# Holding back expert loads until the first gathers have landed, and gathering rows four tiles ahead

## The chip, the cores and the metric

The kernel runs on one core of a Trainium2 chip, as one program launched once. The metric is the device time of that launch in microseconds (us), the median of several runs of the same program on the same inputs. All arrays are in float32 unless a line says otherwise.

## The reference

The input is `x` of shape (2, 1024, 256), which is 2048 tokens of 256 values, with 77 context rows for each of the two sequences. Eight residual steps follow, in four pairs of an attention step and a feed-forward step; each adds its result to `x`, and its input is the layer norm of `x`.

```
x = x + L0_xattn(norm(x), ctx)      # softmax over the queries
x = x + L0_ffn(norm(x))             # dense, with quantised weights and activations
x = x + L1_xattn(norm(x), ctx)      # 16 heads, with its own feed-forward inside
x = x + L1_ffn(norm(x))             # 16-head self-attention, then 8 experts, top 2 of each token
x = x + L2_xattn(norm(x), ctx)
x = x + L2_ffn(norm(x))             # 8 experts, every expert whose sigmoid is over 0.5
x = x + L3_xattn(norm(x), ctx)
x = x + L3_ffn(norm(x))             # 8 experts, the best one of each token
```

An expert is `act(t @ W1 + b1) @ W2 + b2` with W1 of 256x1024 and W2 of 1024x256; its result is multiplied by the token's weight for that expert and summed over the chosen experts.

## The kernel before

Each step is a stage with its own block of instructions on every engine. The change is in one function, `routed_layer`, which runs three times: for the top-2 layer (semaphores and tiles named m1), the threshold layer (m2) and the top-1 layer (m3). Here they are called the first, second and third routed stage.

**Routing.** The normed tokens (16 tiles of 128 tokens) are stored to a table in device memory, `scratch_rows`, by four transfers on SyncE's queue (L1940). TensorE turns the tokens and computes the gate. VectorE picks the experts, computes each token's weight for each expert and, with TensorE, a list of tokens for every expert, cut into tiles of 128 places; the last tile of an expert is filled up with a padding id. ScalarE's queue stores the weights beside the tokens' rows in the same table (L2308, 2048 pieces of 32 bytes). The list of ids lands in the tile `ids` (L2245), which raises `ids_done`.

**The loop over tiles.** Every tile belongs to one expert. Its steps on the engines are:

- GpSimd copies 128 ids into a place of `row_ids` (L1984) and issues an indirect DMA, the gather, that brings 128 rows of the table into a place of `rows`, a ring of four (L1987). For the first tiles this is done ahead of the loop (L2011 and L2015), after GpSimd has waited for `stored`, the landing of all five stores into the table, and for `ids_done`.
- TensorE turns the rows (`transpose_rows`, L2074), VectorE copies them to `rowsT` (L2270, or L2266 with gain and shift in the first stage), TensorE multiplies by W1 (`first`, L2083, 32 instructions), ScalarE applies the activation, TensorE multiplies by W2 (`second`, L2092, and L2095 for the output bias).
- VectorE copies W1 of the next tile's expert (L2255) and the tile's weights (`weight`, which raises `tail_in`, L2274).
- ScalarE scales the result into a place of `y` (L2331, which raises `y_sb`). GpSimd issues an indirect DMA that adds the 128 rows of `y` to the stream in device memory (L1998). An addition is issued only after the one before it has landed (`y_out`).

TensorE's order is written out by hand: `first(s)`, `transpose_rows(s + 1)`, `second(s - 1)`. GpSimd's order is in `add_rows(s)`: wait until addition s - 1 has landed, gather tile s + 3, wait for `y` of tile s, issue addition s. The loop is unrolled over four pairs of tiles and skips the pairs that the routing left empty. There are 38, 68 and 20 tiles in the three stages.

**The experts.** W1 and W2 of an expert are 1 MB each. The first two (first stage) or three (second and third) are loaded during the attention ahead of the stage (`fetched`); SyncE loads the others in the routed stage, two experts in flight, and begins as soon as its four stores of the table are issued.

**Filler.** While TensorE has nothing to do it multiplies the identity (`keep_busy`, L76). Fourteen such matmuls stand between `ids_done` and the first `transpose_rows`; each is two of the instructions that the profile counts.

Of the kernel before, what the change touches and what calls it, by code (L numbers as in the profile page):

```python
# [10 lines left out]
I32 = mybir.dt.int32  # L11
# [3 lines left out]
P = 128  # L15
BATCH, SEQ, D = 2, 1024, 256
TOK = BATCH * SEQ
# [7 lines left out]
FB = FF // P  # L25
# [1795 lines left out]
def routed_layer(core, name, kind, src, stream, func, params, route, experts, fetched, ready, last=False):  # L1821
# [11 lines left out]
    with ExitStack() as ctx:  # L1833
# [15 lines left out]
        if not local:  # L1849
# [4 lines left out]
        ids = sb("ids", [P, COLS + 3], I32)  # L1854
        ends_of, room_of = sb("ends_of", [P, 1]), sb("room_of", [P, 1])
        lf = sb("lf", [1, 1])
        expert, column, last_pair_sb = sb("expert", [1, S + 2], I32), sb("column", [1, S + 3], I32), sb("last_pair", [1, 1], I32)
# [3 lines left out]
        weight, row_ids, bias = sb("weight", [P, RING]), sb("row_ids", [P, RING], I32), sb("bias", [P, 2, FB])  # L1861
# [34 lines left out]
            sem("ids_in"), sem("ids_seen"), sem("tail"), sem("y_free"), sem("y_taken"), sem("acc_in"))  # L1896
        rT_mm, rT_sb, h_mm, hT_sb, y_mm, y_sb, w1_in = (
# [12 lines left out]
        def each_pair(eng, last_pair, step, finish=None):  # L1910

            with eng.Fori(0, S // 2 // PAIRS) as g:
                with eng.If(g * PAIRS <= last_pair):
                    for q in range(PAIRS):
                        step(g * PAIRS + q, q % 2)
                    if finish is not None:
                        with eng.If(last_pair < g * PAIRS + PAIRS):
                            finish()

        def each_tile(eng, step):  # L1920

            last_pair = eng.value_load(last_pair_sb[:], min_val=0, max_val=S // 2 - 1)

            def pair(i, h):
                with eng.If(i <= last_pair):
                    for u in range(2):
                        step(i * 2 + u, u, 2 * h + u, i, last_pair)

            each_pair(eng, last_pair, pair)
            return last_pair  # L1930

        @block.sync
        def _(sp):
# [7 lines left out]
            for e in range(fetched):  # L1941
                arrived(e)
            for e in range(fetched, fetched + 2):
                experts.fetch(sp, e)
# [11 lines left out]
        def _(pool):  # L1956
# [21 lines left out]
            def gather(s, v):  # L1978

                if local:  # L1980
                    at = pool.value_load(column[0:1, bass.ds(s, 1)], min_val=0, max_val=COLS + 1)
                else:
                    at = s
                pool.tensor_copy(row_ids[:, v:v + 1], ids[:, bass.ds(at, 1)]).then_inc(ids_in, 1)  # L1984
                pool.wait_ge(ids_in, s + 1)
                pool.sem_inc(ids_seen, 1)
                pool.indirect_dma_start(rows[:, v, :], None, table, bass.IndirectOffsetOnAxis(ap=row_ids[:, v:v + 1], axis=0),  # L1987
                                        bounds_check=TOK, oob_is_err=False).then_inc(rows_in[v], 16)

            def add_rows(s, u, v, i, last_pair):  # L1990

                pool.wait_ge(y_out, s * 16 + 16)
                pool.sem_inc(y_free, 1)
                with pool.If(i + u < last_pair):
                    gather(s + 3, (v + 3) % RING)
                pool.wait_ge(y_sb, s + 3)
                pool.sem_inc(y_taken, 1)
                pool.indirect_dma_start(stream, bass.IndirectOffsetOnAxis(ap=row_ids[:, v:v + 1], axis=0), y[:, v, :], None,  # L1998
# [4 lines left out]
            if local:  # L2003
                pool.wait_ge(where_done, 1)
                starts = [pool.value_load(column[0:1, s:s + 1], min_val=0, max_val=COLS + 1) for s in range(3)]
            pool.wait_ge(stored, STORED)
            pool.wait_ge(ids_done, 1)
            for s in range(3):
                with (pool.If(last_pair > 0) if s == 2 else nullcontext()):
# [14 lines left out]
        def _(pe):  # L2024
# [81 lines left out]
            core.keep_busy(pe, SPARE_BANK, 14)  # L2106
# [23 lines left out]
        def _(dve):  # L2130
# [130 lines left out]
            def step(s, u, v, i, last_pair):  # L2261
# [18 lines left out]
        def _(act):  # L2280
# [52 lines left out]
            def tile(s, u, v, i, last_pair):  # L2333
# [761 lines left out]
```

## Time and profile before

| what | value |
|---|---|
| median of 3 runs | 2172.44 us (2170.95 to 2173.98) |
| profiled execution, its own time | 2175.15 us |
| its span, first to last instruction | 2173.4 us, of which 1.75 us of its time lie outside |
| TensorE matmul busy | 2013.2 us, 93% of the span |
| GpSimd busy | 728.1 us, 33% |
| VectorE busy | 1038.0 us, 48% |
| mean granted TensorE clock | 0.973 of full speed |
| data moved | 150.45 MB, mean 69 GB/s |
| first routed stage | about 914.9 to 1245 us of the span |
| second routed stage | about 1292 to 1849 us |
| third routed stage | about 1978.4 us to the end |

Times of the trace are microseconds from the first instruction. Busy time counts an engine's own instructions; waits, branches and the issue of a DMA by SyncE or ScalarE don't count. A DMA has a time from its issue to its landing, which is when its semaphore is raised. The granted clock is TensorE's, 1.00 for 2.4 GHz and 0.50 for 1.2 GHz.

### The profile page before, as it was taken

The page shows a single profiled execution, that of the slowest core. Times are in us where ns is not written, and L with a number is a line of the kernel's source. Part 1 is how long each engine was busy: PE and PEld are TensorE (multiplying, and loading weights), DVE is VectorE, ACT ScalarE, POOL GpSimd, SP SyncE. Part 2 cuts the span into 40 slices and gives each one's busy share as a digit, 9 for nine tenths or more (in the row PEclk, how much of TensorE's full clock was granted, in tenths as well). Part 3 has the DMA queues.
Part 4 walks back from the last instruction along what each step waited for, and adds up shares of the span by engine and source line. Part 5 has one row for each costly group of instructions (what it writes and reads, how often), then busy time and mean ns, then how long its engine had stood idle before and what let it go on. Part 6 is the DMA issues. An engine that isn't in the chain of part 4 may idle for free. (4 is left out here: it accounts for less than half of the span.)

```text
span 2173.4 us, 39673 instructions
## 1 busy us (share of the span) xinstructions
PE 2013.2 (93%) x12648; PEld 1474.7 (68%) x12652; DVE 1038.0 (48%) x2419; ACT 933.5 (43%) x1932; POOL 728.1 (33%) x814
## 2 busy tenths in 40 slices
PE   6899999888999999879999888999999998898998
PEld 5566656642322232469999777999999998566897
DVE  6885853667877785442322164222222221685221
ACT  1422652257777778413333241333333333363232
POOL 0123973410000000314444341334334333684243
PEclk9999999999999999989999988999999999899999
DMA  5003300053111112271222266222222212506211
GB/s 167 20 1 129 125 5 1 1 168 53 40 50 43 38 40 96 76 248 34 34 33 35 44 227 201 38 35 35 35 33 36 37 32 30 184 21 218 67 33 25
DMA packets 125501, 150.45 MB, mean 69 GB/s; under 512 B 28278, under 2 KB 105943, under 8 KB 125389
## 3 DMA queue, kind: packets, MB, share of 16 engines
q1 hardware_dynamic: 94477, 116.41, 16.8%
q0 software_dynamic: 24288, 31.81, 9.0%
q10 hardware_dynamic: 6624, 0.79, 0.3%
q8 instruction: 64, 1.05, 0.2%
q14 instruction: 48, 0.39, 0.1%
HBM read 113.33 MB, written 37.38 MB: 69 GB/s over the span
## 5 line engine op out<-in xcount | busy, mean ns | idle before, releaser
L2083 PE MATMUL banks<-m_rowsT,x_normT 128*128 128x128 f32 x4032 | 476.1, 277 | 4.9 <-DVE m_rowsT L2270 2.4
L2083 PEld LDWEIGHTS banks<-m_rowsT,x_normT 128*128 128x128 f32 x4032 | 465.5, 193 | 21.6 <-issue 4.6
L2092 PE MATMUL banks<-m_experts,m_hT 128*128 x2016 | 456.8, 380 | 0.0
L2092 PEld LDWEIGHTS banks<-m_experts,m_hT 128*128 128x128 f32 x2016 | 373.2, 190 | 47.2 <-issue 0.2
L2321 ACT ACTIVATE m_hT<-banks,m_bias 128x128 f32<-128x128 f32 x848 | 242.4, 369 | 258.9 <-PE banks L2083 258.9
L2789 ACT ACTIVATE sh_pT<-banks 128x1024 f32<-128x1024 f32 x256 | 250.8, 1023 | 26.5 <-PE banks L2746 26.4
L2270 DVE COPY m_rowsT<-banks 128x256 f32<-128x256 f32 x88 | 37.4, 425 | 435.9 <-PE banks L2074 435.9
L2331 ACT ACTIVATE m_y<-banks,m_weight 128x256 f32<-128x256 f32 x126 | 59.8, 474 | 355.6 <-PE banks L2095 291.6
L2813 DVE TENSOR_REDUCE sh_mhalf<-banks 128x1 f32<-128x512 f32 x308 | 194.3, 684 | 35.6 <-PE banks L2694 35.4
L1998 POOL DMA_INDIRECT scratch_acc<-m_y,m_row_ids x106 | 169.3, 1597 | 122.0 <-issue 61.9
L2255 DVE TENSOR_SCALAR x_normT<-m_experts 128x2048 f32 x129 | 158.3, 1227 | 75.2 <-issue 71.0
L2746 PE MATMUL banks<-sh_qs,sh_ks 99*128 99x512 bf16 x512 | 152.8, 383 | 9.7 <-ACT sh_pT L2789 7.5
L1987 POOL DMA_INDIRECT m_rows<-scratch_rows,m_row_ids x117 | 124.8, 1066 | 100.7 <-POOL m_row_ids L1984 97.1
L1984 POOL COPY m_row_ids<-m_ids 128x1 int32 x117 | 41.7, 356 | 328.9 <-DMA scratch_acc<-m_y,m_row_ids 219.4
L76 PE MATMUL banks<-ident 128*128 128x256 f32 x398 | 104.7, 416 | 38.5 <-PEq L1833 24.3
L2694 PE MATMUL banks<-sh_ks,sh_qs 96*128 96x512 bf16 x410 | 135.5, 386 | 0.0
L2736 PE MATMUL banks<-sh_pT,sa_vh 128*17 128x512 f32 x1024 | 132.0, 597 | 1.2 <-ACT sh_pT L2789 1.2
L2681 POOL TENSOR_TENSOR x_norm<-x_norm,sp_bo 128x256 f32<-128x256 f32 x16 | 11.6, 724 | 354.0 <-DVE sh_m L2823 354.0
L2746 PEld LDWEIGHTS banks<-sh_qs,sh_ks 99*128 99x128 bf16 x512 | 41.3, 98 | 116.2 <-ACT sh_pT L2789 51.0
L76 PEld LDWEIGHTS banks<-ident 128*128 128x128 f32 x398 | 81.1, 210 | 55.1 <-issue 42.1
L2266 DVE TENSOR_SCALAR m_rowsT<-banks,m1p_gain,m1p_shift 128x128 f32<-128x128 f32 x76 | 27.7, 406 | 189.6 <-PE banks L2074 189.6
L2694 PEld LDWEIGHTS banks<-sh_ks,sh_qs 96*128 96x128 bf16 x410 | 40.1, 98 | 76.8 <-DVE sh_mhalf L2813 35.7
(411 smaller groups left out, 2757.5 us busy)
## 6 DMA issues: line engine op xcount, KB each, us to landing
m_experts<-L_W SPq DMA_DIRECT2D x32, 1024.0 KB, 10.7
m_experts<-L1f_W SPq DMA_DIRECT2D x16, 1024.0 KB, 9.4
a_bt<-bias SPq DMA_DIRECT2D x16, 616.0 KB, 3.8
scratch_parts<-sp_part SPq DMA_DIRECT2D x48, 128.0 KB, 1.9
scratch_rows<-x_norm SPq DMA_DIRECT2D x12, 512.0 KB, 3.4
sh_ks<-scratch_parts SPq DMA_DIRECT2D x93, 64.0 KB, 2.2
sh_qs<-scratch_parts SPq DMA_DIRECT2D x90, 64.0 KB, 2.3
scratch_acc<-x_resid SPq DMA_DIRECT2D x8, 512.0 KB, 2.9
```

The lines of the kernel that those rows point to most:

```text
L76: pe.matmul(self.ps[:, bank, 0:2 * P], self.ident[:], self.ident[:].unsqueeze(1).broadcast_to([P, 2, P]), start=True, stop=True)
L1987: pool.indirect_dma_start(rows[:, v, :], None, table, bass.IndirectOffsetOnAxis(ap=row_ids[:, v:v + 1], axis=0), bounds_check=TOK, oob_is_ ...
L1998: pool.indirect_dma_start(stream, bass.IndirectOffsetOnAxis(ap=row_ids[:, v:v + 1], axis=0), y[:, v, :], None, bounds_check=TOK - 1, oob_i ...
L2083: mm = pe.matmul(ps[:, H_BANK[u] + f // 4, f % 4 * P:(f % 4 + 1) * P], w1_tile[:, u, k, f * P:(f + 1) * P], rowsT[:, u, k, :], start=(k == ...
L2092: mm = pe.matmul(ps[:, Y_BANK[u], 0:D], hT[:, u, f, :], experts.w2[:, bass.ds(slot_of(e), 1), f, :], start=(f == 0), stop=(f == FB - 1 and ...
L2255: ins = dve.tensor_scalar(w1_tile[:, u, :, :], experts.w1[:, bass.ds(slot_of(e), 1), :, :].rearrange("p e k f -> p (e k) f"), 0.0, None, A ...
L2321: ins = act.activation(hT[:, u, f, :], ps[:, H_BANK[u] + c, j * P:(j + 1) * P], func, bias=bias[:, u, f:f + 1])
L2694: pe.matmul(ps[:, bank["a", s, c], :], qs[u][0:SR, h, t * P:(t + 1) * P], keys, start=True, stop=True).then_inc(a_mm, 1)
L2736: mm = pe.matmul(ps[32 * g:32 * g + DK + 1, O_BANK, :], vh[:, b * KT + k, head, :], pT[:, (2 * k + h) % 4, half, :], start=(k == 0), stop= ...
L2746: mm = pe.matmul(ps[:, B_BANK + 2 * (n % 2) + half, :], ks[u][:, h, k * P:(k + 1) * P], qs[u][:, h, half * CH:(half + 1) * CH], start=True ...
L2789: act.activation(pT[:, n % 4, :, :], ps[:, B_BANK + 2 * (n % 2):B_BANK + 2 * (n % 2) + 2, :], ACT.Exp, scale=DK ** -0.5).then_inc(exp_done, 1)
L2813: dve.tensor_reduce(mhalf[:, s % 2, half, col:col + 1], ps[:, bank["a", s, c], :], AX, ALU.max).then_inc(a_max, 1)
```

## The change

SyncE waits, before it loads the first of the remaining experts, until the gathers of the tiles 0 and 1 have landed. Four gathers instead of three are issued ahead of the loop (the third and the fourth only where there is more than one pair). Inside the loop `add_rows(s)` now first waits until the weights of tile s have been copied (`tail_in`), gathers tile s + 4 into the place of `rows` that tile s had, and only then waits for the landing of addition s - 1. Since addition s still reads its ids while those of tile s + 4 are written, `row_ids` has eight places instead of four; the index that the helpers pass is one of eight, and the other engines take it modulo four. The list of ids has one more column of padding. The filler ahead of the first tile is 5 matmuls instead of 14.

```diff
--- before.py
+++ after.py
@@ -1851,14 +1851,14 @@
         chosen = sb("chosen", [P, NT + 1, EXPERTS], BF16)
         tiles_of, start, ends = sb("tiles_of", [P, EXPERTS]), sb("start", [P, EXPERTS]), sb("ends", [P, EXPERTS])
         tile_at, lane_at = sb("tile_at", [P, G, NT], F16), sb("lane_at", [P, G, NT], F16)
-        ids = sb("ids", [P, COLS + 3], I32)
+        ids = sb("ids", [P, COLS + 4], I32)
         ends_of, room_of = sb("ends_of", [P, 1]), sb("room_of", [P, 1])
         lf = sb("lf", [1, 1])
-        expert, column, last_pair_sb = sb("expert", [1, S + 2], I32), sb("column", [1, S + 3], I32), sb("last_pair", [1, 1], I32)
+        expert, column, last_pair_sb = sb("expert", [1, S + 2], I32), sb("column", [1, S + 4], I32), sb("last_pair", [1, 1], I32)
 
         rows, rowsT = sb("rows", [P, RING, ROW]), sb("rowsT", [P, 2, KD, P])
         hT, y = sb("hT", [P, 2, FB, P]), sb("y", [P, RING, D])
-        weight, row_ids, bias = sb("weight", [P, RING]), sb("row_ids", [P, RING], I32), sb("bias", [P, 2, FB])
+        weight, row_ids, bias = sb("weight", [P, RING]), sb("row_ids", [P, 2 * RING], I32), sb("bias", [P, 2, FB])
         opened, warm = sb("opened", [P, 1]), sb("warm", [P, 1])
 
         early = rows[:].rearrange("p v d -> p (v d)")
@@ -1894,6 +1894,7 @@
         parts_done, lanes_done, table_mm, ids_done = sem("parts"), sem("lanes"), sem("table_mm"), sem("ids")
         ids_in, ids_seen, tail_in, y_free, y_taken, acc_in = (
             sem("ids_in"), sem("ids_seen"), sem("tail"), sem("y_free"), sem("y_taken"), sem("acc_in"))
+        row_free = sem("row_free")
         rT_mm, rT_sb, h_mm, hT_sb, y_mm, y_sb, w1_in = (
             sem(n) for n in ("rT_mm", "rT_sb", "h_mm", "hT_sb", "y_mm", "y_sb", "w1_in"))
         y_out = core.lasting_semaphore(f"{name}_y_out")
@@ -1912,7 +1913,7 @@
             with eng.Fori(0, S // 2 // PAIRS) as g:
                 with eng.If(g * PAIRS <= last_pair):
                     for q in range(PAIRS):
-                        step(g * PAIRS + q, q % 2)
+                        step(g * PAIRS + q, q)
                     if finish is not None:
                         with eng.If(last_pair < g * PAIRS + PAIRS):
                             finish()
@@ -1921,10 +1922,10 @@
 
             last_pair = eng.value_load(last_pair_sb[:], min_val=0, max_val=S // 2 - 1)
 
-            def pair(i, h):
+            def pair(i, q):
                 with eng.If(i <= last_pair):
                     for u in range(2):
-                        step(i * 2 + u, u, 2 * h + u, i, last_pair)
+                        step(i * 2 + u, u, 2 * q + u, i, last_pair)
 
             each_pair(eng, last_pair, pair)
             return last_pair
@@ -1940,6 +1941,8 @@
                 sp.dma_start(table[g * CH:(g + 1) * CH, 0:D].rearrange("(t p) d -> p t d", p=P), xn[:, 4 * g:4 * g + 4]).then_inc(stored, 16)
             for e in range(fetched):
                 arrived(e)
+            for v in range(2):
+                sp.wait_ge(rows_in[v], 16)
             for e in range(fetched, fetched + 2):
                 experts.fetch(sp, e)
             for e in range(fetched, EXPERTS):
@@ -1975,38 +1978,40 @@
             pool.wait_ge(pairs_done, 3)
             pool.tensor_copy(last_pair_sb[:], lf[:]).then_inc(pairs_done, 1)
 
-            def gather(s, v):
+            def gather(s, w):
 
                 if local:
                     at = pool.value_load(column[0:1, bass.ds(s, 1)], min_val=0, max_val=COLS + 1)
                 else:
                     at = s
-                pool.tensor_copy(row_ids[:, v:v + 1], ids[:, bass.ds(at, 1)]).then_inc(ids_in, 1)
+                pool.tensor_copy(row_ids[:, w:w + 1], ids[:, bass.ds(at, 1)]).then_inc(ids_in, 1)
                 pool.wait_ge(ids_in, s + 1)
                 pool.sem_inc(ids_seen, 1)
-                pool.indirect_dma_start(rows[:, v, :], None, table, bass.IndirectOffsetOnAxis(ap=row_ids[:, v:v + 1], axis=0),
-                                        bounds_check=TOK, oob_is_err=False).then_inc(rows_in[v], 16)
-
-            def add_rows(s, u, v, i, last_pair):
-
+                pool.indirect_dma_start(rows[:, w % RING, :], None, table, bass.IndirectOffsetOnAxis(ap=row_ids[:, w:w + 1], axis=0),
+                                        bounds_check=TOK, oob_is_err=False).then_inc(rows_in[w % RING], 16)
+
+            def add_rows(s, u, w, i, last_pair):
+
+                with pool.If(i + 1 < last_pair):
+                    pool.wait_ge(tail_in, s + 3)
+                    pool.sem_inc(row_free, 1)
+                    gather(s + RING, (w + RING) % (2 * RING))
                 pool.wait_ge(y_out, s * 16 + 16)
                 pool.sem_inc(y_free, 1)
-                with pool.If(i + u < last_pair):
-                    gather(s + 3, (v + 3) % RING)
                 pool.wait_ge(y_sb, s + 3)
                 pool.sem_inc(y_taken, 1)
-                pool.indirect_dma_start(stream, bass.IndirectOffsetOnAxis(ap=row_ids[:, v:v + 1], axis=0), y[:, v, :], None,
+                pool.indirect_dma_start(stream, bass.IndirectOffsetOnAxis(ap=row_ids[:, w:w + 1], axis=0), y[:, w % RING, :], None,
                                         bounds_check=TOK - 1, oob_is_err=False, compute_op=ALU.add).then_inc(y_out, 16)
 
             pool.wait_ge(pairs_done, 4)
             last_pair = pool.value_load(last_pair_sb[:], min_val=0, max_val=S // 2 - 1)
             if local:
                 pool.wait_ge(where_done, 1)
-                starts = [pool.value_load(column[0:1, s:s + 1], min_val=0, max_val=COLS + 1) for s in range(3)]
+                starts = [pool.value_load(column[0:1, s:s + 1], min_val=0, max_val=COLS + 1) for s in range(RING)]
             pool.wait_ge(stored, STORED)
             pool.wait_ge(ids_done, 1)
-            for s in range(3):
-                with (pool.If(last_pair > 0) if s == 2 else nullcontext()):
+            for s in range(RING):
+                with (pool.If(last_pair > 0) if s >= 2 else nullcontext()):
                     at = starts[s] if local else s
                     pool.tensor_copy(row_ids[:, s:s + 1], ids[:, bass.ds(at, 1)]).then_inc(ids_in, 1)
                     if local:
@@ -2103,7 +2108,7 @@
             last_pair = pe.value_load(last_pair_sb[:], min_val=0, max_val=S // 2 - 1)
             pe.sem_inc(rT_mm, 2)
             pe.sem_inc(h_mm, 3)
-            core.keep_busy(pe, SPARE_BANK, 14)
+            core.keep_busy(pe, SPARE_BANK, 5)
 
             transpose_rows(0, 0, 0)
             first(0, 0)
@@ -2258,7 +2263,8 @@
                     ins = dve.tensor_scalar(bias[:, u, :], b1_sb[:, bass.ds(e, 1), :].rearrange("p e f -> p (e f)"), 0.0, None, ALU.add)
                 ins.then_inc(w1_in, 1)
 
-            def step(s, u, v, i, last_pair):
+            def step(s, u, w, i, last_pair):
+                v = w % RING
                 e = dve.value_load(expert[0:1, bass.ds(s, 1)], min_val=0, max_val=EXPERTS - 1)
                 dve.wait_ge(rT_mm, s + 3)
                 if affine:
@@ -2330,7 +2336,8 @@
                 act.wait_ge(tail_in, s + 3)
                 act.activation(y[:, v, :], ps[:, Y_BANK[u], 0:D], ACT.Copy, scale=weight[:, v:v + 1]).then_inc(y_sb, 1)
 
-            def tile(s, u, v, i, last_pair):
+            def tile(s, u, w, i, last_pair):
+                v = w % RING
                 activations(s, u)
                 with (nullcontext() if u else act.If(i > 0)):
                     weigh(s - 1, 1 - u, (v - 1) % RING)
```

## Rows read from the trace of the kernel before

**Rows 1.** Page, part 1: engine, busy us, share of the span, instructions.

```profile
PE 2013.2 (93%) x12648; PEld 1474.7 (68%) x12652; DVE 1038.0 (48%) x2419; ACT 933.5 (43%) x1932; POOL 728.1 (33%) x814
```

**Rows 2.** Chain that ended last, third routed stage: start us, us, what.

```profile
2006.01 6.46 DMA m_rows<-scratch_rows,m_ids
```

**Rows 3.** Timeline, first routed stage: start, us, engine, line, op, tiles, count, idle before.

```profile
941.66 0.20 DVE L2245 TENSOR_SCALAR m_ids<-banks 128x40 int32<-128x40 f32 x1 [1.81 <-PE banks L2066]
...
942.92 7.82 PE L76 MATMUL banks<-ident 128*128 128x256 f32 x28 [1.37 <-issue]
...
947.05 0.19 POOL L2011 COPY m_row_ids<-m_ids 128x1 int32<-128x1 int32 x1 [12.57 <-DMA scratch_rows<-x_norm]
...
955.40 5.87 PE L2083 MATMUL banks<-m_rowsT,x_normT 128*128 128x128 f32 x32 [0.82 <-DVE m_rowsT L2266]
...
962.49 3.83 PE L2083 MATMUL banks<-m_rowsT,x_normT 128*128 128x128 f32 x32 [1.00 <-ACT m_hT L2321]
```

**Rows 4.** Line L2308 (ScalarE's store of the routing weights): issue to landing.

```profile
DMA to landing us min/median/max: 12.8/14.6/15.0
```

**Rows 5.** DMA queues from 920.81 to 954: packets, MB, share of 16 engines.

```profile
q10 hardware_dynamic: 2064, 0.07, 3.5%
```

**Rows 6.** Line L1987 (gathers inside the loop): issue to landing.

```profile
DMA to landing us min/median/max: 2.8/2.9/5.9
```

**Rows 7.** Timeline, third routed stage, TensorE.

```profile
2000.76 7.96 PE L76 MATMUL banks<-ident 128*128 128x256 f32 x28 [1.16 <-DVE m_ids L2245]
...
2013.72 5.78 PE L2083 MATMUL banks<-m_rowsT,x_normT 128*128 128x128 f32 x32 [0.52 <-DVE m_rowsT L2270]
...
2020.41 3.83 PE L2083 MATMUL banks<-m_rowsT,x_normT 128*128 128x128 f32 x32 [0.69 <-DVE m_rowsT L2270]
```

**Rows 8.** Windows, first routed stage: busy us by engine, granted clock, DMA share, GB/s.

```profile
943.00:946.00 3.00, 3.00 (x7) 2.41 (x8) 1.31 (x2) 0.00 (x0) 0.00 (x0) 0.50 1.05 379
947.00:950.00 3.00, 3.00 (x16) 2.64 (x15) 0.00 (x0) 0.00 (x0) 2.11 (x4) 1.00 1.03 395
956.00:959.00 3.00, 3.00 (x16) 3.00 (x16) 1.05 (x3) 0.00 (x0) 0.00 (x0) 0.50 1.07 353
```

**Rows 9.** Timeline, second routed stage.

```profile
1327.03 0.19 POOL L2011 COPY m_row_ids<-m_ids 128x1 int32 x1 [15.60 <-DVE m_ids L2245]
...
1327.64 8.30 PE L76 MATMUL banks<-ident 128*128 128x256 f32 x28 [1.26 <-DVE m_ids L2245]
1328.07 1.61 POOL L2015 DMA_INDIRECT m_rows<-scratch_rows,m_row_ids  x1 [0.86 <-POOL m_row_ids L2011]
1328.33 1.23 DVE L2255 TENSOR_SCALAR x_normT<-m_experts 128x2048 f32 x1 [1.54 <-PEq L2104]
...
1336.68 3.84 PE L2083 MATMUL banks<-m_rowsT,x_normT 128*128 128x128 f32 x32 [0.52 <-DVE m_rowsT L2270]
...
1341.43 3.83 PE L2083 MATMUL banks<-m_rowsT,x_normT 128*128 128x128 f32 x32 [0.69 <-DVE m_rowsT L2270]
```

**Rows 10.** Line L2074 (row transposes): idle before it, by releaser (us, times).

```profile
  DMA m_rows<-scratch_rows,m_ids: 14.7, 4
  DMA m_rows<-scratch_rows,m_row_ids: 3.1, 9
```

**Rows 11.** Timeline, third routed stage, the steady loop.

```profile
2086.62 1.06 POOL L1987 DMA_INDIRECT m_rows<-scratch_rows,m_row_ids  x1 [0.88 <-POOL m_row_ids L1984]
...
2086.95 0.47 ACT L2331 ACTIVATE m_y<-banks,m_weight 128x256 f32<-128x256 f32 x1 [3.16 <-PE banks L2092]
...
2088.32 1.60 POOL L1998 DMA_INDIRECT out<-m_y,m_row_ids  x1 [0.64 <-issue]
...
2090.24 0.38 PE L2074 MATMUL banks<-ident,m_rows 128*128 128x128 f32 x2
...
2094.19 0.47 ACT L2331 ACTIVATE m_y<-banks,m_weight 128x256 f32<-128x256 f32 x1 [3.16 <-PE banks L2092]
```

**Rows 12.** Page, part 6: DMA issues of the experts.

```profile
m_experts<-L_W SPq DMA_DIRECT2D x32, 1024.0 KB, 10.7
```

## The prediction

> **What bounds the kernel now.** I read the page's busy shares first: TensorE's matmuls are busy for 93% of the span [rows 1], so what is to be had is in its holes. The second view is the idle time ahead of the row transposes, the place where TensorE needs a gather: 14.7 us before gathers issued ahead of the loop and 3.1 us, in nine waits, before those of the loop [rows 10]. The third is the chain and the timeline at the start of a routed stage. In the third stage the first gather is issued at 2006.01 and lands after 6.46 us [rows 2]; in the first stage the ids were written by 941.86, yet GpSimd copied them at 947.05, released by a store into `scratch_rows` [rows 3]. The last view is the steady loop [rows 11], in which one `y` follows another after 7.24 us (7.36 in the other two stages, which also add a bias with L2095): the gather issued at 2086.62 lands at about 2089.5 and TensorE wants its rows at 2090.24, 0.7 us later. The loop itself runs at TensorE's pace, so GpSimd's 33% [rows 1] is worth nothing but for the moments at which a row comes late.
>
> **The change, part by part.**
>
> *Experts held until two gathers have landed.* The store of the weights takes 12.8 to 15.0 us [rows 4] for 64 KB; its queue, q10, had 2064 packets in 33.2 us, whose own time is 3.5% of that, 1.2 us on each engine [rows 5], while the engines were full (share 1.05 at 379 GB/s [rows 8]). With no expert load beside it I take the landing at 2.9 us, a gather's undisturbed landing [rows 6], from below, and 8 us from above; between them nothing changes, because in the first stage the store is issued at 947.05 - 15.0 = 932.0 and has until 941.9. So in stages one and three the gather starts when the ids are there, as it does now in stage two, where the ids released the copy [rows 9]. First stage: copy 0.2 us after the ids at 942.1, gather 1.04 us later as in [rows 9], at 943.1, landed after 2.9 us instead of about 6 at 946.0. Third stage: the filler begins 1.06 us after the ids (942.92 - 941.86 [rows 3]), so the ids are there at 1999.7 [rows 7]; copy at 1999.9, gather at 2000.9, landed by 2003.8.
>
> The Trainium skill, "DMA: Bandwidth & Descriptors", section "Issuing engines are not separate DMA queues", says that transfers issued by different engines run on the same 16 DMA engines and interleave. By that rule both landings shrink once the loads are away, as 2.9 against 6.46 us already suggests; were the queues apart, the store would still end at 947.05, and the sum would be that of rival B below.
>
> *Filler of 5 matmuls instead of 14.* Once rows come early, the filler decides. Its 14 matmuls run 7.82, 8.30 and 7.96 us [rows 3, 9, 7], the first part at half clock (0.50 from 943 to 946, 1.00 from 947 to 950 [rows 8]). With a fast matmul of 0.45 us and a slow one of 0.90, the three durations say that 3.1, 4.1 and 3.4 us of them are slow (3.1 / 0.90 + 4.72 / 0.45 = 14, and so on). Five matmuls then take 3.8, 4.3 and 3.9 us and end at 946.7, 1331.9 and 2004.7, each just after the landing of the first rows (946.0, about 1328.07 + 3.5 = 1331.6, 2003.8). In stage two this is the whole gain.
>
> *The first tile's clock.* Today TensorE waits after the filler in stages one and three, its clock falls (0.50 from 956 to 959 [rows 8]) and the first 32 matmuls take 5.87 and 5.78 us instead of 3.83 [rows 3, 7]. Without that wait I expect the run of stage two: first matmuls 0.74 us after the filler (1336.68 - 1335.94), those of tile 1 4.75 us later [rows 9]; in stage one 0.3 us more for each, since VectorE evacuates with two instructions.
>
> Start of tile 1's matmuls: first stage 946.7 + 0.74 + 0.3 + 4.75 + 0.3 = 952.8 against 962.49, 9.7 us earlier; second 1331.9 + 0.74 + 4.75 = 1337.4 against 1341.43, 4.0; third 2004.7 + 5.5 = 2010.2 against 2020.41, 10.2. Together 23.9 us. From there on the tiles follow at the same pace.
>
> *Gathers four tiles ahead, before the wait for the addition.* A gather starts more than one tile earlier, so the 3.1 us in nine waits [rows 10] go; between 2.2 and 3.7 us, since some waits hide in the next instruction. I take 3.1. Nothing is late next: TensorE is full.
>
> *Costs.* One gather more ahead of the loop puts GpSimd's release of `y_free` 1.4 us (2 us in stage two) later, at about 6.2 us after the first copy, in stage two 1335.8; VectorE's weight copy of tile 0 wants it at 1334.6 and TensorE wants VectorE again at 1336.5, so it is hidden, by less than 1 us; uncovered it costs 1 us once. Per tile GpSimd gets a wait and an increment, some 0.1 us, in slack: its addition comes 1.37 us after `y` [rows 11] whether or not the gather stands before it. SyncE has nothing queued behind its new wait but the loads. They begin about 1334 and 2005 (in stage one 947.5) instead of about 20 us earlier; an expert of 2 MB needs 10.7 us with two in flight [rows 12], thus one each 5.4 us, and a tile 7.25 us, so even an expert per tile would be kept up with: tile 3 copies its W1 at about 2017, expert 3 has landed at 2016. Zero, and at worst 1 us in stage three. Additions under the loads land later than the usual; four places of `y` take that up. The clock's rise may come later in the new filler than it did; bounds 0 and 2.0 us a stage (5.87 - 3.83), I take 0.4 for each, 1.2.
>
> Sum: 23.9 + 3.1 - 1.2 = 25.8 us. The profiled execution took 2175.15 us, 2.7 more than the median of the runs; from the median 2172.44 - 25.8 = 2146.6, rounded 2147.
>
> **The rivals.**
>
> A. *The short filler leaves the clock low*: 5 matmuls end before it has risen, and the first tile of each stage runs at 1.2 GHz as today. For it: the slow part of the filler was 3.1 to 4.1 us, and the new one lasts hardly longer. Against: work follows at once. Price 2.0 us for each stage, 6: 2153.
>
> B. *The store still holds the first gathers*: it is slow for its 2048 pieces and not for the loads beside it. Then stage one gains 953.9 - 950.9 = 3.0 us (landing alone), stage three 3.6, stage two 4.0, the loop 3.1: 13.7, and 2159. Against: the 1.2 us of [rows 5].
>
> C. *It doesn't show*: an expert that is needed early, or additions delayed under the loads, give back later what the start wins, so that only the loop's 3 us remain: 2169. Against: a full TensorE can't lose time that nobody waits for.
>
> D. *Slower*: GpSimd's moved work now falls beside VectorE's W1 copy. In stage two the gather issue beside L2255 took 1.61 us [rows 9], not 1.06 [rows 11]. If this stretches each tile so that an addition isn't issued within 7.36 us of the one before, GpSimd sets the pace. There are 125 tile periods in the loops: from 25.8 / 125 = 0.21 us a tile the kernel is slower, and at 0.3 us it loses 37.5 - 25.8 = 12, 2184. Against: addition (3.8 us to landing), wait and issue make some 5.5 us a tile. The Trainium skill, "DMA: Bandwidth & Descriptors", section "SWDGE vs HWDGE vs iDMA", has GpSimd write descriptors to rings in SBUF, from which VectorE's two-port mode shuts it out. The 1.61 us agrees with it; it would have to hit every tile by more than the slack of 1.8 us to give the 2184.
>
> **How the numbers follow.** Forecast 2147 with 0.73; A 0.09, B 0.08, C 0.04, D 0.04, and 0.02 for a larger gain (a whole clock phase won more, 2141). The range takes in A and B and, below, the bounds of the loop's term and of the clock: 2140 to 2159, which leaves out about 1 in 10. What a measurement of this kernel can tell from no change is 0.2%, 4.3 us. Faster by more: all but D and half of C, 0.93; within it 0.03; slower 0.04.
>
> **What would show it.** In the profile after: in stages one and three the copy L2011 is released by `m_ids` and not by `scratch_rows`; the store L2308 lands in under 8 us; the first gathers land in about 3 us; L2083 of tile 0 takes 3.8 us in all stages; the filler has 10 instructions and ends about when the rows land; line L2074 waits less than 1 us in the loop; the period of the tiles stays 7.36 (7.25) us. I am wrong if tile 0 still starts at half clock (A), if the copy still waits for the store (B), if L2255 waits for an expert (C), or if the period grows (D).

## The result, and the profile after

The changed kernel took 2146.72 us, the median of 4 runs (2145.42 to 2153.23), against 2172.03 us for the kernel before, run beside it (4 runs, 2170.95 to 2173.98): a ratio of 0.9875 (95% interval 0.9851 to 0.9899). The forecast was 2147. The profiled execution took 2146.70 us, its span is 2144.9 us, 28.5 less than the 2173.4 of before, and the mean granted clock is 0.975 (before 0.973).

The first view is the page's busy time by engine, to be read against [rows 1]: TensorE's matmuls take 19.3 us less, of which the 27 filler matmuls that went make up some 12 (0.45 us each), and fill 93% of a shorter span.

```profile
PE 1993.9 (93%) x12594; PEld 1462.5 (68%) x12598; DVE 1045.7 (49%) x2419; ACT 932.4 (43%) x1932; POOL 718.5 (33%) x814
```

The timeline of the first routed stage of the changed kernel (start, us, engine, line, operation, tiles, count, idle before) answers to [rows 3]; L2245, L2011, L2083 are now L2250, L2016, L2088.

```profile
938.84 0.20 DVE L2250 TENSOR_SCALAR m_ids<-banks 128x40 int32<-128x40 f32 x1 [1.81 <-PE banks L2071]
939.18 0.19 POOL L2016 COPY m_row_ids<-m_ids 128x1 int32<-128x1 int32 x1 [7.52 <-DVE m_ids L2250]
940.04 1.78 POOL L2020 DMA_INDIRECT m_rows<-scratch_rows,m_ids  x1 [0.68 <-issue]
...
940.10 4.05 PE L76 MATMUL banks<-ident 128*128 128x256 f32 x10 [1.37 <-issue]
...
943.98 0.38 PE L2079 MATMUL banks<-ident,m_rows 128*128 128x128 f32 x2
...
945.10 0.37 SPq L395 DMA_DIRECT2D m_experts<-L1f_W  x1
...
945.18 3.84 PE L2088 MATMUL banks<-m_rowsT,x_normT 128*128 128x128 f32 x32 [0.82 <-DVE m_rowsT L2272]
...
950.24 3.83 PE L2088 MATMUL banks<-m_rowsT,x_normT 128*128 128x128 f32 x32 [1.00 <-ACT m_hT L2327]
```

GpSimd's copy is released by the ids and no longer by the store (0.34 us after them instead of 5.4). The first rows are there when the filler of ten instructions ends, and the loads (L395) begin only behind them. Tile 0 runs at full clock (3.84 us). Tile 1's W1 matmuls begin 11.40 us after the ids' instruction instead of 962.49 - 941.66 = 20.83 [rows 3].

The same view of the second stage, for [rows 9]:

```profile
1315.31 0.29 DVE L2250 TENSOR_SCALAR m_ids<-banks 128x128 int32<-128x128 f32 x1 [1.35 <-PE banks L2071]
1315.83 0.19 POOL L2016 COPY m_row_ids<-m_ids 128x1 int32 x1 [15.56 <-DVE m_ids L2250]
...
1316.45 4.61 PE L76 MATMUL banks<-ident 128*128 128x256 f32 x10 [1.25 <-DVE m_ids L2250]
1316.90 1.58 POOL L2020 DMA_INDIRECT m_rows<-scratch_rows,m_row_ids  x1 [0.88 <-POOL m_row_ids L2016]
...
1320.85 0.63 PE L2079 MATMUL banks<-ident,m_rows 128*128 128x128 f32 x2
...
1322.00 5.61 PE L2088 MATMUL banks<-m_rowsT,x_normT 128*128 128x128 f32 x32 [0.52 <-DVE m_rowsT L2276]
...
1328.60 3.83 PE L2088 MATMUL banks<-m_rowsT,x_normT 128*128 128x128 f32 x32 [0.78 <-DVE m_rowsT L2276]
```

Here the filler ran at half clock to its end, and so did the first part of tile 0, which took 5.61 us. The windows of that stage show it (columns: stretch, length, busy of TensorE, its weight loads, VectorE, ScalarE and GpSimd, then the granted clock, the share of the DMA engines and GB/s):

```profile
1317.00:1320.00 3.00, 3.00 (x9) 2.37 (x8) 1.32 (x2) 0.00 (x0) 2.20 (x3) 0.50 0.15 45
1323.00:1326.00 3.00, 3.00 (x18) 3.00 (x17) 0.95 (x3) 0.18 (x1) 1.41 (x2) 0.54 0.85 239
1329.00:1332.00 3.00, 3.00 (x29) 3.00 (x29) 1.28 (x3) 1.14 (x4) 0.00 (x0) 1.00 1.06 375
```

The third stage, for [rows 7]:

```profile
1983.79 0.18 DVE L2250 TENSOR_SCALAR m_ids<-banks 128x24 int32<-128x24 f32 x1 [1.41 <-PE banks L2071]
1984.11 0.18 POOL L2016 COPY m_row_ids<-m_ids 128x1 int32<-128x1 int32 x1 [4.76 <-DVE m_ids L2250]
...
1984.84 3.92 PE L76 MATMUL banks<-ident 128*128 128x256 f32 x10 [1.16 <-DVE m_ids L2250]
...
1988.59 0.38 PE L2079 MATMUL banks<-ident,m_rows 128*128 128x128 f32 x2
...
1989.49 3.84 PE L2088 MATMUL banks<-m_rowsT,x_normT 128*128 128x128 f32 x32 [0.52 <-DVE m_rowsT L2276]
...
1994.24 3.83 PE L2088 MATMUL banks<-m_rowsT,x_normT 128*128 128x128 f32 x32 [0.69 <-DVE m_rowsT L2276]
```

Of the two views by line, the store of the weights (L2314) answers to [rows 4], and the idle time ahead of the row transposes (L2079) to [rows 10], 14.7 and 3.1 us before:

```profile
DMA to landing us min/median/max: 3.0/3.0/4.3
```

```profile
  issue: 0.2, 1
```

**Where the 28.5 us of the span are.** A routed stage is cut here into its start (from the ids' instruction to tile 1's first W1 matmul) and its loop (from there to the last tile's first W1 matmul), both read from the timelines.

| us | start, stages 1, 2, 3 | loop, stages 1, 2, 3 |
|---|---|---|
| before | 20.83, 14.93, 20.70 | 265.96, 489.28, 132.41 |
| changed | 11.40, 13.30, 10.45 | 265.06, 485.77, 130.51 |
| gained | 9.4, 1.6, 10.3 = 21.3 | 0.9, 3.5, 1.9 = 6.3 |

The 0.9 us that remain lie outside these stretches: 1229.3 us of the span before and 1228.4 in the changed kernel. Over the thirteen profiles of this case, whose kernels hardly differ there, that time lies between 1226.3 and 1233.9 us, so the stretches of the table say more than the totals. In the loops before, single tiles followed late (in the second stage tiles 9, 27, 41, 56 and 58, after 7.6 to 8.3 us instead of 7.36); the changed kernel has none.

### The profile page after: what moved, and what is told of

It reads as the page before. It is cut to its first block and busy times, and to the rows that moved or that the text cites. A ratio compares the mean times of both kernels' runs of the same rounds, so it can differ in the third digit from the quotient of the medians.

```text
span 2144.9 us, 39790 instructions
## 1 busy us (share of the span) xinstructions
PE 1993.9 (93%) x12594; PEld 1462.5 (68%) x12598; DVE 1045.7 (49%) x2419; ACT 932.4 (43%) x1932; POOL 718.5 (33%) x814
## 5 line engine op out<-in xcount | busy, mean ns | idle before, releaser
L2088 PE MATMUL banks<-m_rowsT,x_normT 128*128 128x128 f32 x4032 | 473.0, 276 | 4.3 <-DVE m_rowsT L2276 2.5
L2088 PEld LDWEIGHTS banks<-m_rowsT,x_normT 128*128 128x128 f32 x4032 | 463.6, 193 | 18.8 <-DVE m_rowsT L2276 1.7
L2003 POOL DMA_INDIRECT scratch_acc<-m_y,m_row_ids x106 | 172.0, 1623 | 403.0 <-ACT m_y L2337 366.5
L2260 DVE TENSOR_SCALAR x_normT<-m_experts 128x2048 f32 x129 | 167.8, 1301 | 74.6 <-issue 69.8
L2753 PE MATMUL banks<-sh_qs,sh_ks 99*128 99x512 bf16 x512 | 151.9, 381 | 10.2 <-ACT sh_pT L2796 8.0
L76 PE MATMUL banks<-ident 128*128 128x256 f32 x344 | 93.1, 422 | 38.0 <-PEq L1833 23.8
L76 PEld LDWEIGHTS banks<-ident 128*128 128x128 f32 x344 | 70.7, 213 | 53.1 <-issue 41.6
L2825 DVE CUSTOM_DVE_ANT_0 sh_rise<-banks,sh_rise 128x512 f32<-128x512 f32 x102 | 68.7, 689 | 44.8 <-ACT sh_rise L2784 44.6
```

The costliest lines, as they stand in the source:

```text
L76: pe.matmul(self.ps[:, bank, 0:2 * P], self.ident[:], self.ident[:].unsqueeze(1).broadcast_to([P, 2, P]), start=True, stop=True)
L2088: mm = pe.matmul(ps[:, H_BANK[u] + f // 4, f % 4 * P:(f % 4 + 1) * P], w1_tile[:, u, k, f * P:(f + 1) * P], rowsT[:, u, k, :], start=(k == ...
L2260: ins = dve.tensor_scalar(w1_tile[:, u, :, :], experts.w1[:, bass.ds(slot_of(e), 1), :, :].rearrange("p e k f -> p (e k) f"), 0.0, None, A ...
L2753: mm = pe.matmul(ps[:, B_BANK + 2 * (n % 2) + half, :], ks[u][:, h, k * P:(k + 1) * P], qs[u][:, h, half * CH:(half + 1) * CH], start=True ...
```

## The experiments

Theory 1 (the prediction's): each part gives what it gives by itself, the hold and the short filler the starts, the gathers the waits in the loop. Rivals: B and C of the prediction, and that the loop's part comes only in company of the others. Ten more kernels ran, and the changed one again: the first four of the table in one batch, the next four in a second, the last three in a third. All ratios are against the kernel before in the same batch; in the first batch its 28 runs lay between 2168.98 and 2181.50 us, so a single run says little, and the median and the interval count. In the second column of this table the gains of the six stretches above are added up, so that it can be seen how far a trace and a timing agree.

| kernel | stretches, us gained | timed, us gained | ratio (95%) |
|---|---|---|---|
| hold alone | 11.1 - 21.7 = -10.6 | -8.5 | 1.0041 (1.0023 to 1.0058) |
| short filler alone | -0.5 - 1.4 = -1.9 | 0.5 | 0.9996 (0.9984 to 1.0008) |
| hold, short filler | 21.2 - 26.6 = -5.4 | -2.9 | 1.0010 (0.9993 to 1.0027) |
| gathers alone | -0.6 + 6.3 = 5.7 | 4.9 | 0.9977 (0.9961 to 0.9993) |
| four ahead, behind the landing | 23.0 + 0.4 = 23.4 | 23.5 | 0.9897 (0.9880 to 0.9915) |
| three ahead, before the landing | 22.8 + 2.4 = 25.2 | 24.4 | 0.9890 (0.9861 to 0.9920) |
| changed, no hold | -1.5 + 6.3 = 4.8 | 8.2 | 0.9967 (0.9957 to 0.9977) |
| changed, filler 14 | 11.2 + 6.3 = 17.5 | 14.7 | 0.9938 (0.9920 to 0.9955) |
| changed, held for the store | 5.7 + 6.3 = 12.0 | 13.8 | 0.9929 (0.9904 to 0.9954) |
| clock kept up | 24.0 + 6.3 = 30.3 | 31.5 | 0.9858 (0.9835 to 0.9881) |
| changed, once more | 23.0 + 6.3 = 29.3 | 30.7 | 0.9856 (0.9833 to 0.9879) |

**The hold alone.** The kernel before, with SyncE's wait.

```diff
             for e in range(fetched):
                 arrived(e)
+            for v in range(2):
+                sp.wait_ge(rows_in[v], 16)
```

> The kernel before with nothing but SyncE's wait for the first two gathers. Main theory (the start is won by the hold and by the shorter filler, each of which needs the other): the store lands before the ids, the first rows land about 3 us after their issue, but the filler of 14 still runs until about 950.7 and 2008.7, so tile 1's matmuls start 5.6 us earlier in the first stage and 6.2 us in the third, the second is unchanged: 11.8 us off, 2160. Rival (the hold alone is the gain at the start, the filler costs nothing): some 21 us off, 2151. Rival (the store is slow for its own 2048 pieces): L2011 in stages one and three still released by scratch_rows, at most 7 us off, 2165 or more.

Measured: 2183.22 us against 2174.74, slower by 0.4%, where all three theories had a gain. The starts came as expected (15.01, 15.86, 14.50 us, a gain of 11.1), but the loops lost 6.5, 8.0 and 7.1 us, nearly all of it at tile 4, which followed tile 3 after 13.92, 15.17 and 14.86 us. TensorE's idle time ahead of the row transposes, 14.7 and 3.1 us before, is all in the loop now:

```profile
  DMA m_rows<-scratch_rows,m_row_ids: 34.3, 13
```

**The short filler alone** (`keep_busy` 14 to 5).

> The kernel before with a filler of 5 matmuls instead of 14. Main theory: stages one and three still wait for the store, so nothing comes off there (the rows arrive as late, TensorE at half clock, as before); only the second stage, where the filler ended last, starts earlier, 1.6 us if its first tile then runs at half clock and 3.9 us if not: 2168 to 2170.5. Rival (the shorter filler is the gain at the start): 2155 or less.

Measured: 2174.26 us, no change, where 1.6 to 3.9 us were expected. The starts are 21.31, 14.88 and 20.75 us. In stages one and three the rows are what is waited for; in stage two tile 0 starts 1.6 us earlier but at half clock, and tile 1 starts when it did.

**Hold and short filler, gathers as before.**

> Hold and filler of 5 together, gathers three ahead and behind the addition's landing as before. Main theory: the whole gain of the starts, 9.4 + 1.6 + 10.2 = 21.3 us as the changed kernel shows it, and the holes of the loop (6.3 us) stay: 2151. The rival that the starts owe part to the fourth gather would leave this above 2153.

Measured: 2177.68 us, no gain at all, where 2151 was expected and the changed kernel gains 25. The starts have the full gain (11.32, 13.30, 10.62 us); the loops lose 8.9, 10.4 and 7.3 us, with tile 4 late by 7 to 10 us in each. The timeline of the first stage of this kernel shows the chain:

```profile
962.59 1.65 POOL L2000 DMA_INDIRECT scratch_acc<-m_y,m_row_ids  x1 [11.75 <-ACT m_y L2333]
...
970.28 0.18 POOL L1986 COPY m_row_ids<-m_ids 128x1 int32 x1 [6.04 <-DMA scratch_acc<-m_y,m_row_ids]
...
971.35 1.09 POOL L1989 DMA_INDIRECT m_rows<-scratch_rows,m_row_ids  x1 [0.88 <-POOL m_row_ids L1986]
...
977.44 0.69 PE L2076 MATMUL banks<-ident,m_rows 128*128 128x128 f32 x2 [5.42 <-DMA m_rows<-scratch_rows,m_row_ids]
...
977.92 2.35 PE L2094 MATMUL banks<-m_experts,m_hT 128*128 x5
```

Addition 0 is issued at 962.59 and lands after 7.32 us, beside expert loads; in the kernel before the last load of the stage landed at 961.42, addition 0 was issued at 971.61, and it landed after 3.72 us. Only then (L1986, "<-DMA scratch_acc") may GpSimd copy the ids of tile 4 and gather them; that gather, slow as well, lands at 977.4, and TensorE, done with all that it had, sits idle for 5.42 us and then starts at half clock (0.55 from 977 to 980). So C's mechanism is real, and it costs all that the start wins, in the order of the kernel before.

**The gathers alone**: the changed kernel without SyncE's wait and with the filler of 14.

> The changed kernel without the hold and with the filler of 14: only the gathers (four ahead, before the wait for the addition's landing, eight places of ids). Theory 1 (a row that is late by a little also takes the lead of TensorE's sequencer, so that the holes at the loop's boundaries belong to it): all tile periods are 7.36 or 7.25 us, 6.3 us off, 2165.7. Theory 2 (only the waits that the profile names go): 3.1 us off, 2169, and single periods of 7.4 to 7.7 us remain without a wait at L2079. The starts stay as before, at 20.8, 14.9 and 20.7 us from the ids to tile 1's matmuls.

Measured: 2169.80 us, 4.9 less than before (interval 1.5 to 8.5 by the ratio), which can't tell theory 1's 6.3 us from theory 2's 3.1. The trace can: the loops are those of the changed kernel to 0.01 us (265.05, 485.77, 130.51), with no late tile. So the 6.3 us belong to the gathers alone and need no company; the starts are those of before to 0.8 us.

**Four ahead, but behind the addition's landing.** Of the changed kernel, with the gather's block moved back.

```diff
-                with pool.If(i + 1 < last_pair):
-                    ...
-                    gather(s + RING, (w + RING) % (2 * RING))
                 pool.wait_ge(y_out, s * 16 + 16)
                 pool.sem_inc(y_free, 1)
+                with pool.If(i + 1 < last_pair):
+                    ...
+                    gather(s + RING, (w + RING) % (2 * RING))
```

> The changed kernel with the gather of tile s + 4 put back behind the wait for the landing of addition s - 1 (still four ahead, eight places). Theory L (an addition lands in 7 to 8.5 us beside the expert loads, a gather in 6 to 7, and what costs is a gather that is both queued behind such a landing and only three tiles ahead): one tile more of lead is 7.4 us and covers it, by a margin of about 1 us at tiles 5 and 6; 2147 to 2150, period of tile 4 at 7.36. Rival (the wait for the landing alone is the fault): the stall of tile 4 moves to tile 5, 7 us a stage, 2160 or more.

Measured: 2152.18 us (ratio 0.9897), above the expected 2147 to 2150. Tile 4 is on time, as theory L has it: four gathers stand ahead of the loop and the fifth has a tile more of time. But tile 6 is late, by 2.2 us in stage one (after 9.52 us) and by 0.5 and 0.3 in the others. The late tiles of before are back too (in stage two 9, 27, 56 and 58 after 7.72 to 8.14 us), and the loops gain 0.4 us instead of 6.3. Timeline, second stage of this kernel:

```profile
1729.16 1.06 POOL L1990 DMA_INDIRECT m_rows<-scratch_rows,m_row_ids  x1 [0.86 <-POOL m_row_ids L1987]
1730.52 1.60 POOL L2003 DMA_INDIRECT scratch_acc<-m_y,m_row_ids  x1 [0.30 <-issue]
...
1732.98 0.44 PE L2079 MATMUL banks<-ident,m_rows 128*128 128x128 f32 x2 [0.40 <-DMA m_rows<-scratch_rows,m_row_ids]
```

The gather issued at 1729.16 is four tiles ahead in number only. GpSimd itself is a tile behind: from tile 2 to tile 63 of this stage its additions begin 7.8 to 9.1 us after ScalarE has finished their `y`, where nearly all of the changed kernel's begin 0.88 us after it from tile 4 on. So TensorE still waits for that gather at 1732.98.

**Three ahead, but before the landing.**

> The changed kernel with three gathers ahead instead of four, still issued before the wait for the addition's landing. Theory L: the gather of tile 4 stands behind the issue of addition 0 (about 961) and lands at 969.5 where TensorE wants it at 968.8; the gather of tile 6 stands behind addition 2, which waits for addition 1, and is 1 to 2 us late in one or two stages: 2149 to 2153, steady periods of 7.36. Rival (the lead of a tile is what counts): 7 us or more in a stage, 2160 or more.

Measured: 2151.30 us (ratio 0.9890), as expected. The starts are 11.39, 11.68 and 10.61 us, with tile 0 at full clock in all three stages. One or two tiles are late early in each loop (tile 4 of stage one after 8.44 us, tile 5 of stage two after 8.55), none afterwards. Each half of the gather's change alone shrinks the stall of 7 to 10 us at tile 4 to 2.2 us or less at one or two tiles; only both leave no late tile.

**The changed kernel without the hold.**

> The changed kernel without SyncE's wait, filler of 5 kept. Main theory: stages one and three wait for the store again, 20.7 us from the ids to tile 1's matmuls, stage two as in the changed kernel or up to 1.6 us behind it; the loop keeps its 6.3 us. Lost against the changed kernel: 9.4 + 10.2 + 0 to 1.6, which gives 2166 to 2168.

Measured: 2167.53 us (ratio 0.9967), as expected; stores land after 13 to 15 us again, and the starts of stages one and three are those of before (21.03 and 20.86 us). Stage two's was expected at 13.3 to 14.9 us and took 16.02, with tile 0 partly at half clock (5.99 us).

**The changed kernel with the filler of 14.**

> The changed kernel with the filler of 14. The starts become those of the kernel with nothing but the hold, 15.0, 15.9 and 14.5 us from the ids to tile 1's matmuls instead of 11.4, 13.3 and 10.5; tile 0 runs at full clock in all three stages. 10.2 us lost: 2157. The rival that the clock gives the filler back (full clock earlier) would leave less than 6 us.

Measured: 2161.02 us (ratio 0.9938), above the expected 2157. The starts are 15.27, 15.63 and 14.36 us, as expected: against the changed kernel's first profile the short filler is worth 3.9, 2.3 and 3.9 us, 10.1 in all. By the timings it is 10.6 us (against 25.3 gained in the first comparison) or 16.0 (against 30.7 in the third batch).

**Held for the store alone.**

```diff
-            for v in range(2):
-                sp.wait_ge(rows_in[v], 16)
+            sp.wait_ge(stored, STORED)
```

> The changed kernel with SyncE held only until the five stores into the table have landed (about 932, 1299 and 1980), not until two gathers have. Theory: the hold's worth has two parts, the store (5 us in stages one and three, none in two) and the landing of the gathers. The first part stays, the second goes: the first gathers land in 6 us instead of 3.4, so the start is 2 to 2.6 us later in each stage, and the clock may fall in the longer wait, 0 to 2 us more: 2153 to 2157. The additions meet the loads for a shorter time, which wins nothing, since no tile waits in the changed kernel. Rival (all of the worth is in the store): 2147.

Measured: 2162.25 us (ratio 0.9929), slower than either theory said. The store is as quick as in the changed kernel and GpSimd's copy follows the ids, but the loads begin at 935.43, as soon as the store has landed. That is 7.8 us ahead of the first gather, and they are under way when it is issued (DMA share 1.06 from 943 to 950). Timeline of its first stage:

```profile
935.43 0.37 SPq L395 DMA_DIRECT2D m_experts<-L1f_W  x1
...
942.40 0.19 POOL L2015 COPY m_row_ids<-m_ids 128x1 int32<-128x1 int32 x1 [7.51 <-DVE m_ids L2249]
943.26 1.79 POOL L2019 DMA_INDIRECT m_rows<-scratch_rows,m_ids  x1 [0.68 <-issue]
...
943.78 0.37 SPq L395 DMA_DIRECT2D m_experts<-L1f_W  x1
...
950.50 0.69 PE L2078 MATMUL banks<-ident,m_rows 128*128 128x128 f32 x2 [3.06 <-DMA m_rows<-scratch_rows,m_ids]
...
952.01 6.23 PE L2087 MATMUL banks<-m_rowsT,x_normT 128*128 128x128 f32 x32 [0.82 <-DVE m_rowsT L2271]
```

The gather lands after 7.20 us (6.78 and 6.47 in the other stages; 3.35 to 3.73 in the changed kernel), TensorE waits 3.06 us behind its filler, its clock falls (0.50 from 952 to 955), and tile 0 takes 6.23 us. Of the 22.8 us that the hold gives the starts of the changed kernel, the wait for the gathers has 6.0, 3.8 and 5.9; the store has 3.6, -1.1 and 4.6 (this kernel against the one without the hold).

**Clock kept up.** Can the half clock at tile 0 of stage two be had back? The filler behind the matmuls of the ids' placing goes from 6 to 8, two new ones stand behind the matmuls of the table, and the last filler is 4 in stage two and 7 in the others.

> The changed kernel with TensorE's filler spread so that its clock is up when the ids are there: 8 instead of 6 ahead of the table's matmuls, 2 behind them, and then 4 in the threshold layer and 7 in the others instead of 5. Theory: the first rows bound the start in stages one and three (0.2 us earlier at most), and in stage two tile 0 runs at full clock more often (11.6 us from the ids to tile 1 instead of 13.3): 1 to 2 us off, 2145, inside the noise of the totals; the profile decides by the stretches from the ids. Rival: the filler added ahead of the ids delays them in the third stage, and nothing is won, 2147 to 2149.

> The changed kernel once more, beside the other two on the same chip, as the measure for them: about 25 us under the kernel before.

Measured: 2144.55 and 2145.28 us, ratios 0.9858 and 0.9856, the same. The changed kernel is 30.7 us under its neighbour here, against 25.3 in the first comparison; the intervals of the two ratios (0.9833 to 0.9879 and 0.9851 to 0.9899) overlap. Start of stage two 10.66 us against 11.53 us; in this second profile the changed kernel itself had tile 0 nearly at full clock. TensorE's rows of that second profile, second stage:

```profile
1324.69 3.91 PE L2088 MATMUL banks<-m_rowsT,x_normT 128*128 128x128 f32 x32 [0.52 <-DVE m_rowsT L2276]
...
1329.52 0.71 PE L2088 MATMUL banks<-m_rowsT,x_normT 128*128 128x128 f32 x4 [0.69 <-DVE m_rowsT L2276]
```

So the 5.61 us of the first profile is not what that stage always costs, and a filler made for it brings nothing that can be measured.

## Why the prediction was right, and where not

**Starts of stages one and three** (forecast 9.7 and 10.2, less 0.4 each for the clock; 9.4 and 10.3 measured). Step by step as written: copy after the ids, gathers landed after 3.73 and 3.37 us (forecast 2.9) instead of 5.9 and 6.5, filler of 4.05 and 3.92 us (forecast 3.8 and 3.9), tile 0 at full clock. The store landed after 3.0, 3.0 and 4.3 us, at the lower bound; B falls. The Trainium skill, "DMA: Bandwidth & Descriptors", section "Issuing engines are not separate DMA queues", says that transfers interleave on the same 16 DMA engines whichever engine issued them. The trace agrees: with SyncE's loads gone, ScalarE's store took 3.0 us instead of 15.0.

**Start of stage two** (forecast 4.0 less 0.4; 1.6 measured, 3.4 in the second profile of the same kernel). Rival A's mechanism took place in this stage of this execution, and again in the profile of hold and short filler (5.61 us); in the profiles of four behind, three ahead and the changed kernel's second, the same stage had tile 0 at 3.84 to 3.91 us. The allowance was 0.4 us; tile 0's W1 matmuls alone took 1.8 more than at full clock (5.61 - 3.83), and 0.1 more (3.91) in the second profile. The size of this term changes from one execution to the next.

**The loop's term** (3.1, "between 2.2 and 3.7") is the one mis-sized: 6.3 us. This is the step that was wrong: the prediction took GpSimd's 33% as slack and priced only the waits at the row transposes. Rows of the kernel before, second stage, GpSimd:

```profile
1758.72 1.60 POOL L1998 DMA_INDIRECT scratch_acc<-m_y,m_row_ids  x1 [0.31 <-issue]
1763.54 0.18 POOL L1984 COPY m_row_ids<-m_ids 128x1 int32 x1 [3.22 <-DMA scratch_acc<-m_y,m_row_ids]
1764.59 1.06 POOL L1987 DMA_INDIRECT m_rows<-scratch_rows,m_row_ids  x1 [0.86 <-POOL m_row_ids L1984]
1765.95 1.60 POOL L1998 DMA_INDIRECT scratch_acc<-m_y,m_row_ids  x1 [0.30 <-issue]
```

From one addition to the next are 7.23 us in series (issue, landing, copy, gather), and TensorE's tile takes 7.36. GpSimd was at 33% and had 0.1 us to spare: a delay was made up by some 0.1 to 0.3 us a tile at most, and what was left made tiles late. After one delayed addition in that stage (that of tile 54, 2.19 us behind the end of its `y`) the next two stood 1.91 and 0.92 us behind, the usual being 0.88; what brought it back was mostly TensorE being late itself, at tile 58. (The prediction's 1.37 us counts from the start of ScalarE's instruction.) With the gather in front, three ahead, a delay of the same size there was gone at the next tile. In the changed kernel the landing covers the gather, and GpSimd catches up from delays far larger:

```profile
976.24 2.54 POOL L2003 DMA_INDIRECT scratch_acc<-m_y,m_row_ids  x1 [4.78 <-issue]
...
984.56 1.62 POOL L2003 DMA_INDIRECT scratch_acc<-m_y,m_row_ids  x1 [3.65 <-issue]
...
989.44 1.60 POOL L2003 DMA_INDIRECT scratch_acc<-m_y,m_row_ids  x1 [1.13 <-issue]
...
996.12 1.60 POOL L2003 DMA_INDIRECT scratch_acc<-m_y,m_row_ids  x1 [2.58 <-ACT m_y L2337]
```

984.56 to 989.44 is 4.9 us for one tile, issue and landing (3.85 us) included. The sentence that the share "is worth nothing" was wrong; the kernels with the gather behind the landing keep late tiles even four ahead, those with it in front lose them.

**"Additions under the loads land later than the usual; four places of `y` take that up"** was right, but for a reason that was not seen. In the changed kernel the first two or three additions of a stage take 6.93 to 8.53 us to land, against 5.1 at most before, and no row comes late: the gathers are past them. The line of the additions (L2003) of the changed kernel:

```profile
DMA to landing us min/median/max: 2.7/3.8/8.5
```

But that holds by virtue of the order alone. In the old order the loops lose 26.6 us under the same loads (hold and short filler). The prediction set rival C aside with "a full TensorE can't lose time that nobody waits for"; somebody did wait, the gather of tile 4. It also gave the hold as a gain by itself; alone it loses 8.5 us, and the parts timed alone (-8.5, 0.5, 4.9) add up to -3 where together they gain 25.

**D** falls: the periods are 7.36 and 7.25 us. Its mechanism was there all the same. In the changed kernel's profile 13 issues took over a fifth longer than usual, gathers up to 2.11 us instead of 1.02 to 1.06 and three additions 2.52 to 2.54 instead of 1.60, and each lay over a W1 copy of VectorE in part or whole:

```profile
976.24 2.54 POOL L2003 DMA_INDIRECT scratch_acc<-m_y,m_row_ids  x1 [4.78 <-issue]
977.47 1.23 DVE L2260 TENSOR_SCALAR x_normT<-m_experts 128x2048 f32 x1 [0.33 <-issue]
```

Not every overlap cost something (the addition at 984.56, 1.62 us, lay over a copy too), and a GpSimd that needs 4.9 us in 7.36 could take it. The other slips change nothing: the loops have 123 tile periods and not 125, and an expert's W2 landed 5.8 to 7.7 us after the one before it and not 5.4, which no tile waited for.

So 2147 was met with the right mechanism at the starts, and with stage two 2.0 too high and the loop 3.2 too low, errors that partly cancel. By the trace the stretches gained 27.6 us against the 25.8 of the sum. That the median came within 0.3 us is luck: the same kernel gained 25.3 us in one comparison and 30.7 in the other.

## What to carry to other kernels

Before a load is moved, ask what will land beside it in its new place, and who is queued behind that landing: the price of a transfer's neighbours may come a tile or four later. An engine at a third of its time can still be a series of landings as long as the pace, so add up its chain from one issue to the next rather than read its share. Parts of a change that cover each other must be timed with one part left out, not only alone.

## What the runs showed of the hardware

Short transfers took far longer beside expert loads: the 64 KB store in 2048 pieces went from 3.0 to 15.0 us, gathers of 128 rows from 2.9 to between 5.7 and 7.7, additions from 3.8 to between 6.4 and 8.5. The indirect issue itself stretched beside VectorE's W1 copy, from 1.60 to 2.54 us at most for an addition. Open: why the late tiles of the old order are the same ones in every kernel (9, 27, 56, 58 in stage two); that the order of GpSimd's chain lets them be late is shown, the delays that start them are not explained. Open too is why the same filler leaves tile 0 of stage two at half clock in one execution and not in the next.
